# Three pairs of cms chunks with their down projections by seven products per pair

## The chip, the cores and the metric

The kernel runs on one core of one Trainium2 chip. The metric is the device time of one execution in microseconds (us). TensorE is called PE here (its sequencer starts one matmul after the other), VectorE DVE, ScalarE ACT, GpSimd POOL and SyncE SP. SP issues nearly all the transfers.

## The reference, cut to what matters

Four blocks run one after the other over x (4 batches of 512 tokens of width 512). Blocks 0 and 2 are the "cond" blocks, 1 and 3 are adapters with a layer norm. The part in question is the cms perceptron of a cond block:

```python
attn_out = jnp.einsum('btT,bTd->btd', attn, v) @ Wp + bp
cms_out = jax.nn.gelu(attn_out @ cW1 + cb1, approximate=False) @ cW2 + cb2   # 512 -> 2048 -> 512
cms_out = cms_out + target_embed
concat = jnp.concatenate([attn_out, cms_out], axis=-1)
modifier = jax.nn.gelu(concat @ mW1 + mb1, approximate=False) @ mW2 + mb2    # 1024 -> 2048 -> 512
out = jnp.clip(x + cms_out + modifier, 0.0, 1.0)
```

All is fp32.

## The kernel before

**Rounds and slots.** Two batches and one layer pair (a cond block and its adapter) are one round; there are 4 rounds (2 layers x 2 groups of batches). A round has the attention, then 16 slots, then the adapter. The hidden width of 2048 is cut into 8 chunks of 256. Slots 0 to 7 are the chunks of cms, slots 8 to 15 those of the modifier.

**Precision by halves.** Each fp32 operand is held as a high part in fp32r and a low part (the rest). ACT writes the high part with a copy, DVE subtracts it from the original and writes the low part. A product of two such operands is three matmuls (high x high, high x low, low x high), each of 128 x 128 weights by 512 columns, as lines 615 to 617 of `tile` issue them.

**Seven products.** The two batches of a round and the halves of the weights form 2 x 2 block matrices, which are multiplied by seven products instead of eight. The weights' sums S1 to S4 are made by POOL (`sums`, line 551 and on, 128 x 256 each). The products are Q1 to Q7. An up projection of slots 1 to 15 goes that way: seven products of 6 matmuls in the cms slots (A alone), of 12 in the modifier's (A and C). In slots 8 to 14 the down projection does, too (`down_product`): its operands are sums of the hidden tiles, made by POOL (`hidden_sum`, lines 563 to 575, 128 x 512 each), and its results are added up by DVE two tiles at a time (`seven_add`, lines 1474 to 1480). The down projection of the cms slots is plain (`down`): 8 output tiles, each of 2 parts, 48 matmuls a slot, and DVE adds each tile (`down_add`, line 1493).

**A cms slot.** PE goes through Q1, Q5, Q6, Q2, Q7 of chunk n, then the first batch's down projection of chunk n - 1, Q4, Q3, and the second batch's. ACT copies finished products from bank to bank as the start of others (`take`, line 1091), applies the gelu (line 1098), and makes the high parts of hidden tiles (`hidden_hi`, line 1103) and of weights (`split_hi`, line 955). DVE makes the low parts (`hidden_lo`, line 1517; `split_lo`, line 1321), the adds, and the sums of two products (`combine`, line 1504).

**Orders.** Each engine has its own list, written out by hand, and executes it in order; semaphores tie them together. An engine that waits holds up all that stands behind in its list. PE's products wait for `w_lo` (the low part of the weights), for `h_lo` (of the hidden tile) and for `added` (the bank has been drained).

**Weights.** SP loads them into three stage buffers. In the cms slots the up weights of chunk n (A) take stage 0 or 1 by turns and the down weights (D) stage 2. A load waits until the last low part has been made of what the buffer held. From the stage, ACT and DVE write both parts into a ring, from where PE reads.

Of the kernel before, what the change touches and what calls it, by code (L numbers as in the profile page):

```python
# [9 lines left out]
P = 128  # L10
D = 512
T = 512
# [18 lines left out]

BP, CB1, CB2, MB1, MB2 = 0, KT, KT + HID // P, 2 * KT + HID // P, 2 * KT + 2 * HID // P
# [7 lines left out]
LASTS = (CH - 1, SLOTS - 1)  # L40

# [17 lines left out]
UP_ORDER = ((Q1, Q5, Q6, Q2, Q7, Q4, Q3), (Q1, Q5, Q6, Q2, Q3, Q7, Q4))  # L59

DOWN_ORDER = ((Q1, Q5, Q6, Q3, Q7, Q4, Q2), (Q1, Q5, Q6, Q3, Q7, Q2, Q4))

DRAIN = {Q1: (0, 0), Q2: (0, 0), Q5: (1, 2), Q6: (1, 0), Q3: (1, 0), Q7: (1, 2), Q4: (0, 2)}
LAST_DRAIN = {(0, 0): Q2, (0, 2): Q4, (1, 0): Q3, (1, 2): Q7}
FIRST_DRAIN = (Q1, Q5, Q6, Q4)

# [14 lines left out]

RING_A, RING_C, RING_DQ = ring_of("A"), ring_of("C"), ring_of("D")
# [15 lines left out]
HID_SUMS = (T1, T3, T2, T4)  # L98
CMS_T = {T1: 2, T2: 3, T3: 4, T4: 5}
# [14 lines left out]

def seven(n):

    return CH <= n < SLOTS - 1


def amid(n):  # L120

    return CH < n < SLOTS - 1
# [14 lines left out]
DOWN_BEFORE, ROUND_DOWNS = counts(lambda n: PRODUCTS if seven(n) else GROUP * KT)  # L137
HID_BEFORE, ROUND_HIDDEN = counts(lambda n: PRODUCTS if seven(n) else 4)
ROUND_HSUMS = len(HID_SUMS) * (SLOTS - 1 - CH)

SPLIT = ((0, 1, 2, 3), (0, 3, 1, 2))
# [6 lines left out]
def weight_stream():  # L148
# [18 lines left out]
    def down(r, n):  # L167
        pieces.append(((r, "D", n), 2))
        ops.append((r, "D", n))

# [9 lines left out]
    for r in range(ROUNDS):  # L180
# [4 lines left out]
        for n in range(CH):  # L185
            if n and n - 1 not in LASTS:
                down(r, n - 1)
            up(r, n + 1, 0)
            if n in LASTS:
                down(r, n)  # L190
            up(r, n + 1, 1)
# [26 lines left out]
for piece_key, stage_at in PIECES:  # L218

    stage_loads[stage_at] += 2 if piece_key[1] in ("A", "C") else 1  # L220
    STAGE_NTH[piece_key] = stage_loads[stage_at]
    STAGE_FREE[piece_key] = LAST_OP[stage_held[stage_at][-1]] if stage_held[stage_at] else N_FOLD
    stage_held[stage_at].append(piece_key)

SUMMED = []
for sum_r in range(ROUNDS):
    for sum_n in range(1, CH):
        SUMMED.append((sum_r, "A", sum_n))
    SUMMED += [(sum_r, "A", CH), (sum_r, "C", CH)]
# [8 lines left out]
def build(nc, x_t, codes, roles, fold_w, cms_w, mod_w, ada_w, vecs, avecs, out):  # L238
# [3 lines left out]
    with ctx:  # L242
# [18 lines left out]
        vc = place("vc", [P, XTILES, T], F32R)  # L261
        pc = place("pc", [P, GROUP, KT, T], F32, at=vc_at + HI_AT[T3] * tile_bytes)
# [6 lines left out]
        stage = [place(f"stage{n}", [P, STAGE_BLOCKS, BLK]) for n in range(3)]  # L269
        fold_staging = place("fold_staging", [P, 4, PIECE], F32, at=stage_at)  # L270
# [92 lines left out]

# [1447 lines left out]
```

## Time and profile before

| | |
|---|---|
| median of 3 runs | 2157.89 us (2156.2 to 2160.65) |
| the profiled execution, its time | 2156.44 us |
| the profiled execution, span of the trace | 2154.8 us |
| granted clock of TensorE, mean | 0.998 |
| busy: PE, DVE, ACT, POOL | 98%, 71%, 48%, 28% |
| matmuls | 9256 |

The span runs from the first to the last instruction of one execution. Busy times leave out waits and the issue of transfers. Two instructions of one engine that follow each other overlap a little in the records, so that the durations of many add up to slightly more than the busy time. In rows of grouped instructions the numbers after the bar are the busy time in us, the mean of one in ns, and the idle time in front of them.

### The profile page before, as it was taken

Reading aid. Unit: us, or ns where it says so; the run is one execution under the profiler, and the core shown is the slowest. Engines: PE = TensorE matmul, PEld = TensorE weight load, DVE = VectorE, ACT = ScalarE, POOL = GpSimd, SP = SyncE. Lnnn points to the kernel's source line nnn. Section 1 sums busy time; section 2 is a strip of 40 time slices with the busy share of each in tenths; the row PEclk is TensorE's granted clock in tenths of the full one; section 3 lists DMA queues with packets and bytes.
Section 4 is the critical chain, followed back from the end, with each engine's and each line's share of the span. In section 5 each row is a group of like instructions: output and inputs, shape, how many; then the busy total and the mean of one; then the engine's idle time right before and its main releaser. Section 6 shows DMA issues by size and latency. Waiting matters only on the chain.

```text
span 2154.8 us, 24846 instructions
## 1 busy us (share of the span) xinstructions
PE 2105.6 (98%) x9256; PEld 1724.7 (80%) x9256; DVE 1537.7 (71%) x1923; ACT 1042.1 (48%) x1527; POOL 598.7 (28%) x620
## 2 busy tenths in 40 slices
PE   8999999999999999999999999999999999999997
PEld 6888887888788887888877888788887888878884
DVE  4366678776867668876776766977686866787676
ACT  5264445454446444544554544444454644454444
POOL 1001136452001113655000111655400011355420
PEclk9999999999999999999999999999999999999999
DMA  8101131212202112221312111321130211311211
GB/s 304 40 10 59 59 88 49 59 48 78 100 20 88 59 59 69 59 59 59 116 41 88 40 59 42 96 59 59 40 127 20 102 46 59 88 50 59 59 59 39
DMA packets 125767, 146.41 MB, mean 68 GB/s; under 512 B 5952, under 2 KB 100160, under 8 KB 123728
## 3 DMA queue, kind: packets, MB, share of 16 engines
q1 hardware_dynamic: 122912, 130.05, 18.9%
q0 software_dynamic: 1504, 8.49, 1.9%
q10 hardware_dynamic: 1232, 6.29, 0.7%
q8 instruction: 74, 1.21, 0.2%
q14 instruction: 45, 0.37, 0.1%
HBM read 123.84 MB, written 12.58 MB: 63 GB/s over the span
## 4 chain that ended last, share of the span: by engine, by line
PE 85%; DVE 10%; ACT 2%; issue 2%; DMA 0%; SPq 0%; ACTq 0%; DVEq 0%
PE bank L615 28%; PE bank L617 28%; PE bank L616 28%; DVE ring L1321 2%; DVE vc L1363 2%; DVE pc L1493 1%; DVE xa L1358 1%; DVE lsum L1695 1%; ACT ring L955 1%; ACT raw L1098 0%; PE bank L923 0%; DVE xs L1700 0%; DVE xs L1653 0%; DVE xs L1685 0%; DVE raw L1439 0%
## 5 line engine op out<-in xcount | busy, mean ns | idle before, releaser
L1321 DVE TENSOR_TENSOR ring<-stage,ring 128x1024 fp32r<-128x1024 f32 (+1 forms) x312 | 363.4, 1176 | 103.8 <-ACT ring L955 103.6
L551 POOL TENSOR_TENSOR stage<-stage 128x256 f32<-128x256 f32 x120 | 106.3, 886 | 1122.1 <-DMA stage<-cms_w 904.5
L615 PE MATMUL bank<-ph_hi,ring 128*128 128x512 f32 x1048 | 410.6, 392 | 5.4 <-issue 2.4
L617 PE MATMUL bank<-ph_hi,ring 128*128 128x512 f32 x1048 | 407.9, 389 | 0.0
L616 PE MATMUL bank<-ph_lo,ring 128*128 128x512 f32 x1048 | 407.9, 389 | 0.0
L615 PE MATMUL bank<-xa,ring 128*128 128x512 f32 x1016 | 396.0, 390 | 2.9 <-DVE xs L1653 2.1
L617 PE MATMUL bank<-xa,ring 128*128 128x512 f32 x1016 | 395.3, 389 | 0.0
L616 PE MATMUL bank<-xa,ring 128*128 128x512 f32 x1016 | 395.3, 389 | 0.0
L955 ACT ACTIVATE ring<-stage 128x1024 fp32r<-128x1024 f32 (+1 forms) x312 | 296.3, 970 | 111.7 <-PE bank L617 78.3
L615 PEld LDWEIGHTS bank<-ph_hi,ring 128*128 128x128 f32 x1048 | 196.7, 188 | 53.7 <-issue 7.2
L617 PEld LDWEIGHTS bank<-ph_hi,ring 128*128 128x128 f32 x1048 | 196.7, 188 | 41.0
L616 PEld LDWEIGHTS bank<-ph_lo,ring 128*128 128x128 f32 x1048 | 196.8, 188 | 40.8 <-issue 0.7
L1517 DVE TENSOR_TENSOR ph_lo<-raw,ph_hi 128x512 fp32r<-128x512 f32 x312 | 214.8, 711 | 17.4 <-ACT ph_hi L1103 17.3
L615 PEld LDWEIGHTS bank<-xa,ring 128*128 128x128 f32 x1016 | 190.7, 188 | 45.3 <-DVE ring L1321 5.8
L617 PEld LDWEIGHTS bank<-xa,ring 128*128 128x128 f32 x1016 | 190.7, 188 | 39.6
L616 PEld LDWEIGHTS bank<-xa,ring 128*128 128x128 f32 x1016 | 190.8, 188 | 39.4
L615 PE MATMUL bank<-vc,ring 128*128 128x512 f32 x512 | 200.4, 391 | 7.5 <-DVE ring L1321 6.1
L616 PE MATMUL bank<-vc,ring 128*128 128x512 f32 x512 | 199.3, 389 | 0.0
L617 PE MATMUL bank<-vc,ring 128*128 128x512 f32 x512 | 199.2, 389 | 0.0
L1493 DVE TENSOR_TENSOR pc<-bank,pc 128x512 f32<-128x512 f32 x224 | 152.3, 689 | 60.5 <-PE bank L617 60.2
L1103 ACT ACTIVATE ph_hi<-raw 128x512 fp32r<-128x512 f32 x144 | 87.9, 629 | 200.1 <-PE bank L617 198.5
L1504 DVE TENSOR_TENSOR raw<-bank,snap 128x512 f32<-128x512 f32 x112 | 77.2, 689 | 144.6 <-PE bank L617 140.3
(159 smaller groups left out, 3139.6 us busy)
## 6 DMA issues: line engine op xcount, KB each, us to landing
stage<-mod_w SPq DMA_DIRECT2D x128, 256.0 KB, 3.4
stage<-cms_w SPq DMA_DIRECT2D x36, 512.0 KB, 3.6
stage<-mod_w SPq DMA_DIRECT2D x32, 512.0 KB, 4.9
stage<-cms_w SPq DMA_DIRECT2D x56, 256.0 KB, 4.3
fold_staging<-fold_w SPq DMA_DIRECT2D x16, 512.0 KB, 5.2
stage<-folded SPq DMA_DIRECT2D x16, 512.0 KB, 4.3
xs<-pc POOLq DMA_DIRECT2D x8, 1024.0 KB, 8.3
stage<-ada_w SPq DMA_DIRECT2D x16, 512.0 KB, 3.6
```

The lines of the kernel that those rows point to most:

```text
L551: pool.tensor_tensor(part(S1), part(S2), part(A22), ALU.add).then_inc(sums_ready, 1)
L615: pe.matmul(dst, lh, rh, start=start and n == 0, stop=False, skip_group_check=not start)
L616: pe.matmul(dst, lh, rl, start=False, stop=False, skip_group_check=not start)
L617: done = pe.matmul(dst, ll, rh, start=False, stop=n == last, skip_group_check=not start)
L955: act.activation(ring_part(key, 0), staged(key), ACT.Copy).then_inc(w_hi, 1)
L1103: act.activation(ph_hi[:, tile, :], raw[:, tile, :], ACT.Copy).then_inc(h_hi, 1)
L1321: dve.tensor_tensor(ring_part(key, 1), staged(key), f32(ring_part(key, 0)), ALU.subtract).then_inc(w_lo, 1)
L1358: dve.tensor_tensor(xa[:, 8 + 4 * b + k:8 + 4 * b + k + 2, :], src[:, b, k:k + 2, :], f32(xa[:, 4 * b + k:4 * b + k + 2, :]), ALU.subtract ...
L1363: dve.tensor_tensor(block_lo(t, blk, j, n), src, f32(block_hi(t, blk, j, n)), ALU.subtract).then_inc(lo_sem, 1)
L1493: done = dve.tensor_tensor(acc, src, acc, ALU.add)
L1504: dve.tensor_tensor(raw[:, to, :], bank[BANK[q]][:, :], snap[:, 0, :], ALU.add).then_inc(combined, 1)
L1517: done = dve.tensor_tensor(ph_lo[:, at, :], src, f32(ph_hi[:, at, :]), ALU.subtract)
```

## The change

Chunks 0 to 5 of cms are taken in three pairs. The down projection of a pair is one 2 x 2 block product (batches by hidden halves: chunk 2i and chunk 2i + 1) and goes by seven products of 2 tiles x 2 parts x 3 = 12 matmuls. Chunks 6 and 7 keep the plain down projection.

- **PE.** In an odd slot (n = 2i + 1) it goes through Q5, Q1 of the up projection, the pair product Q7 of the pair before, Q6, Q2, pair Q4, Q3, pair Q2, Q7, then pair Q1 of its own pair, Q4, pair Q5. In an even slot: Q5, Q1, pair Q3, Q6, Q2, Q3, Q7, pair Q6, Q4. An odd slot has 102 matmuls (66 in slot 1), an even one 66. Slot 7 finishes pair 2 and does chunks 6 and 7.
- **Hidden sums.** POOL makes T1 to T4 of a pair, 8 sums of 128 x 512. Chunk 2i + 1 has its own hidden tiles `raw_odd`. ACT and DVE split 14 tiles per pair where they split 8. The high part of the second tile of T4, the fourth sum, stands behind the copy of Q6 in ACT's list.
- **Weights.** The pair's down weights are a piece "E" of 7 blocks of 128 x 512 across stages 1 and 2, loaded by 4 transfers of 256 KB (`load_pair`). POOL makes four sums of 128 x 512 of them, ACT and DVE split it in four parts of 2, 1, 2 and 2 blocks. The up weights A of all cms chunks now pass through stage 0 alone, which P holds before A of chunk 1.
- **DVE** drains a product two tiles at a time (`pair_add`), 7 per pair in place of 16 adds.

The core of the diff; the lists of ACT, DVE and PE for the slots:

```diff
-        pieces.append(((r, "A", n), n % 2 if n < CH else 0))
+        pieces.append(((r, "A", n), 0))
...
+            def load_pair(r, n):
+                sp.wait_ge(w_lo, STAGE_FREE[r, "E", n])
+                for c, blocks in ((n - 1, (PAIR_AT[A11], PAIR_AT[S4])), (n, (PAIR_AT[A12], PAIR_AT[A22]))):
...
+                    for m, to in enumerate(blocks):
+                        sp.dma_start(stage_pair[:, to, :].rearrange("p (k n) -> p k n", k=2), src[:, :, m, :]).then_inc(stage_in[1], 16)
...
+                for n in range(1, CH):
+                    i = n // 2
+                    if n % 2 and paired(n):
+                        pair_sum(r, i, T1, 0)
+                        pair_sum(r, i, T1, 1)
+                        sums((r, "A", n + 1))
+                        for j in range(2):
+                            pair_sum(r, i, T3, j)
+                            pair_sum(r, i, T2, j)
+                    elif n % 2 == 0:
+                        pair_sum(r, i - 1, T4, 0)
+                        pair_sum(r, i - 1, T4, 1)
+                        sums((r, "A", n + 1))
+                        if paired(n):
+                            sums((r, "E", n + 1))
...
+            def pair_product(r, i, q):
+                blk, at = OPERAND[q], RING_E[q] * BLK
+                pe.wait_ge(w_lo, W_AT[r, "E", 2 * i + 1, PAIR_GROUP[q]])
+                pe.wait_ge(h_lo, pair_split_at(r, i, blk, 1))
+                before = {Q6: Q1, Q7: Q6, Q4: Q7, Q3: Q5, Q2: Q3}
+                if q in before:
+                    pe.wait_ge(added, pair_down_at(r, i, before[q]))
+                elif i:
+                    pe.wait_ge(added, pair_down_at(r, i - 1, Q4 if q == Q1 else Q2))
...
+            def pair_even(r, n):            # PE
+                i = n // 2 - 1
+                up(r, n, Q5)
+                up(r, n, Q1)
+                pair_product(r, i, Q3)
+                up(r, n, Q6)
+                up(r, n, Q2)
+                up(r, n, Q3)
+                up(r, n, Q7)
+                pair_product(r, i, Q6)
+                up(r, n, Q4)
...
+            def pair_even(r, n):            # ACT
+                i = n // 2 - 1
+                act.wait_ge(down_done, pair_down_at(r, i, Q5))
+                split_hi((r, "E", n - 1, 3))
+                split_hi((r, "A", n, 1))
+                take(r, n, Q1, bank[BANK[Q2]][:, :])
+                pair_t_hi(r, i, T3, 0)
+                pair_b_hi(r, i, B21, 1)
+                pair_t_hi(r, i, T2, 0)
+                take(r, n, Q5, snap[:, 0, :])
+                pair_t_hi(r, i, T3, 1)
+                pair_t_hi(r, i, T2, 1)
+                pair_t_hi(r, i, T4, 0)
+                take(r, n, Q6, bank[BANK[Q3]][:, :])
+                pair_t_hi(r, i, T4, 1)
+                up_turn(r, n, 0)
...
+                split_hi((r, "A", n + 1, 0))
+                up_turn(r, n, 2)
...
+                up_turn(r, n, 3)
...
+                up_turn(r, n, 1)
...
+            def pair_odd(r, n):             # ACT, first lines
+                i = n // 2
+                if i:
+                    split_hi((r, "A", n, 1))
+                if i == 0:
+                    split_hi((r, "E", n, 0))
+                    split_hi((r, "E", n, 1))
+                    act.wait_ge(gelu_done, gelu_at(r, 0, 3))
+                take(r, n, Q1, bank[BANK[Q2]][:, :])
...
+            def pair_even(r, n):            # DVE
+                i = n // 2 - 1
+                pair_add(r, i, Q5)
+                split_lo((r, "E", n - 1, 3))
+                split_lo((r, "A", n, 1))
+                pair_split_lo(r, i, T3, 0)
+                pair_split_lo(r, i, B21, 1)
+                pair_split_lo(r, i, T2, 0)
+                pair_split_lo(r, i, T3, 1)
+                pair_add(r, i, Q3)
+                pair_split_lo(r, i, T2, 1)
+                combine(r, n, C12)
+                pair_split_lo(r, i, T4, 0)
+                combine(r, n, C22)
+                split_lo((r, "A", n + 1, 0))
+                pair_add(r, i, Q6)
+                pair_split_lo(r, i, T4, 1)
+                if paired(n):
+                    pair_split_lo(r, i + 1, B11, 0)
...
+            def pair_odd(r, n):             # DVE
+                i = n // 2
+                if i:
+                    split_lo((r, "A", n, 1))
+                    pair_split_lo(r, i, B11, 1)
+                    pair_add(r, i - 1, Q7)
+                pair_split_lo(r, i, T1, 0)
+                pair_split_lo(r, i, T1, 1)
+                split_lo((r, "E", n, 0))
+                split_lo((r, "E", n, 1))
+                split_lo((r, "A", n + 1, 0))
+                if i:
+                    pair_add(r, i - 1, Q4)
+                combine(r, n, C12)
+                combine(r, n, C22)
+                pair_split_lo(r, i, B22, 0)
+                if i:
+                    pair_add(r, i - 1, Q2)
+                pair_split_lo(r, i, B21, 0)
+                split_lo((r, "E", n, 2))
+                pair_add(r, i, Q1)
+                pair_split_lo(r, i, B22, 1)
```

## Rows read from the trace of the kernel before

**Rows 1.** The page: span, busy times, and the costliest group of matmuls.
```profile
span 2154.8 us, 24846 instructions
...
PE 2105.6 (98%) x9256; PEld 1724.7 (80%) x9256; DVE 1537.7 (71%) x1923; ACT 1042.1 (48%) x1527; POOL 598.7 (28%) x620
...
L615 PE MATMUL bank<-ph_hi,ring 128*128 128x512 f32 x1048 | 410.6, 392 | 5.4 <-issue 2.4
```

**Rows 2.** Stretches: attention, a cms slot, modifier slots; columns in the first line.
```profile
core 0: us, PE busy (x) PEld busy (x) DVE busy (x) ACT busy (x) POOL busy (x), PEclk, DMA share, GB/s
630.00:640.00 10.00, 10.00 (x45) 8.26 (x45) 10.00 (x14) 3.08 (x5) 0.00 (x0) 1.00 0.01 2
...
718.20:738.60 20.40, 20.40 (x92) 16.90 (x91) 12.59 (x18) 9.55 (x15) 3.24 (x4) 1.00 0.17 52
...
880.00:1050.00 170.00, 170.00 (x751) 140.81 (x751) 123.08 (x135) 81.72 (x121) 80.96 (x85) 1.00 0.19 56
```

**Rows 3.** Waits of PE: us in total, times, longest.
```profile
PE bank L615 <- DVE ring L1321: 8.9, 16, 1.5
...
PE bank L654 <- DVE pc L1340: 3.0, 3, 1.0
```

**Rows 4.** Groups of DVE's instructions in two cms slots, 718 to 758.8 us.
```profile
L1493 DVE TENSOR_TENSOR pc<-bank,pc 128x512 f32<-128x512 f32 x17 | 11.7, 690 | 5.7 <-PE bank L617 5.6
L1517 DVE TENSOR_TENSOR ph_lo<-raw,ph_hi 128x512 fp32r<-128x512 f32 x8 | 5.5, 703 | 0.0
L1321 DVE TENSOR_TENSOR ring<-stage,ring 128x1024 fp32r<-128x1024 f32 x4 | 4.9, 1222 | 2.0 <-ACT ring L955 2.0
L1504 DVE TENSOR_TENSOR raw<-bank,snap 128x512 f32<-128x512 f32 x4 | 2.8, 692 | 8.1 <-PE bank L617 8.1
L1321 DVE TENSOR_TENSOR ring<-stage,ring 128x768 fp32r<-128x768 f32 x2 | 1.9, 957 | 0.4 <-ACT ring L955 0.4
```

**Rows 5.** Groups of ACT's instructions in the same two slots.
```profile
L1103 ACT ACTIVATE ph_hi<-raw 128x512 fp32r<-128x512 f32 x10 | 6.0, 628 | 17.2 <-PE bank L617 17.1
L955 ACT ACTIVATE ring<-stage 128x1024 fp32r<-128x1024 f32 x4 | 4.2, 1060 | 1.3 <-PE bank L617 1.3
L1098 ACT ACTIVATE raw<-raw,vec 128x512 f32<-128x512 f32 x4 | 2.9, 716 | 1.6 <-DVE raw L1504 1.6
...
L1091 ACT ACTIVATE bank<-bank 128x512 f32<-128x512 f32 x4 | 2.3, 582 | 1.8 <-PE bank L617 1.8
```

**Rows 6.** A group of POOL's sums of weights in the same two slots.
```profile
L552 POOL TENSOR_TENSOR stage<-stage 128x256 f32<-128x256 f32 x2 | 1.5, 738 | 0.0
```

**Rows 7.** Timeline of DVE and POOL: start, duration in us, then the instruction.
```profile
828.43 4.54 DVE L1363 TENSOR_TENSOR vc<-pc,vc 128x1024 fp32r<-128x1024 f32 x2 [1.13 <-ACT vc L981]
866.62 2.31 DVE L1321 TENSOR_TENSOR ring<-stage,ring 128x1024 fp32r<-128x1024 f32 x1
...
828.46 1.05 POOL L551 TENSOR_TENSOR stage<-stage 128x256 f32<-128x256 f32 x1
...
831.97 1.60 POOL L556 TENSOR_TENSOR stage<-stage 128x256 f32<-128x256 f32 x1
...
866.18 1.67 POOL L575 TENSOR_TENSOR raw<-raw 128x512 f32<-128x512 f32 x1 [1.23 <-DVE ph_lo L1517]
```

**Rows 8.** Timeline of DVE, SP and POOL in a modifier slot, 898 to 908 us.
```profile
898.98 0.94 DVE L1321 TENSOR_TENSOR ring<-stage,ring 128x768 fp32r<-128x768 f32 x1
...
901.10 1.23 DVE L1480 TENSOR_TENSOR xs<-bank,xs 128x1024 f32<-128x1024 f32 x1 [1.18 <-PE bank L617]
...
899.95 1.21 SPq L443 DMA_DIRECT2D stage<-mod_w  x2
...
904.01 0.74 POOL L551 TENSOR_TENSOR stage<-stage 128x256 f32<-128x256 f32 x1 [5.50 <-DMA stage<-mod_w]
...
907.05 1.29 POOL L563 TENSOR_TENSOR raw<-raw 128x512 f32<-128x512 f32 x1
```

**Rows 9.** Timeline of ACT where slot 1 begins.
```profile
677.25 1.14 ACT L1103 ACTIVATE ph_hi<-raw 128x512 fp32r<-128x512 f32 x2
678.29 0.59 ACT L1091 ACTIVATE bank<-bank 128x512 f32<-128x512 f32 x1
```

More of the change, by code:

```diff
@@ L184, in weight_stream @@
         plain(r, "P", 0)
-        for n in range(CH):
-            if n and n - 1 not in LASTS:
-                down(r, n - 1)
-            up(r, n + 1, 0)
-            if n in LASTS:
-                down(r, n)
-            up(r, n + 1, 1)
+        up(r, 1, 0)
+        ops.append((r, "A", 1, 1))
+        for n in range(1, CH - 1):
+            if n % 2 == 0:
+                ops.append((r, "E", n - 1, 3))
+            if n > 1:
+                ops.append((r, "A", n, 1))
+            if n % 2:
+                pair_first(r, n)
+                ops.append((r, "E", n, 1))
+            up(r, n + 1, 0)
+            if n % 2:
+                ops.append((r, "E", n, 2))
+        ops.append((r, "A", CH - 1, 1))
+        down(r, CH - 2)
+        staged_up(r, CH)
+        ops.append((r, "A", CH, 0))
+        down(r, CH - 1)
+        ops += [(r, "C", CH, 0), (r, "A", CH, 1), (r, "C", CH, 1)]
         up(r, CH + 1, 0)
@@ new lines, in pair_add @@
+            def pair_add(r, i, q):
+                b, m = DRAIN[q]
+                acc, src = pc[:, b, m:m + 2, :], pair[int(q in (Q5, Q3, Q2))]
+                minus = q in (Q5, Q7, Q4)
+                dve.wait_ge(down_done, pair_down_at(r, i, q))
+                if q not in PAIR_FIRST_DRAIN:
+                    dve.wait_ge(added, pair_down_at(r, i, {Q2: Q1, Q6: Q3, Q7: Q5}[q]))
+                elif i:
+                    dve.wait_ge(added, pair_down_at(r, i - 1, PAIR_LAST_DRAIN[b, m]))
+                if i == 0 and q in PAIR_FIRST_DRAIN:
+                    dve.wait_ge(attn_lo, (r + 1) * ATT_BUILDS)
+                    for j in range(2):
+                        done = dve.tensor_scalar(acc[:, j, :], src[:, j, :], -1.0 if minus else 1.0,
+                                                 cbias[:, 2 * r + b, m + j:m + j + 1], ALU.mult, ALU.add)
+                elif minus:
+                    done = dve.tensor_tensor(acc, acc, src[:, :, :], ALU.subtract)
+                else:
+                    done = dve.tensor_tensor(acc, src[:, :, :], acc, ALU.add)
+                done.then_inc(added, 1)
@@ L1593, in slot @@
-                up_lo(r, n + 1, 1)
-                if not last:
-                    for m in range(1, KT):
-                        down_add(r, n - 1, 1, m)
+                for m in range(KT):
+                    down_add(r, n - 1, 1, m)
+                hidden_lo(r, n, 3)
+                split_lo((r, "C", n + 1, 0))
+                hidden_lo(r, n, 1)
+                combine(r, n, C12)
+                hidden_lo(r, n, 2)
+                split_lo((r, "A", n + 1, 1))
+                split_lo((r, "C", n + 1, 1))
```

379 lines of the change are left out of this document (277 added, 102 removed).

## The prediction, made before the result was known

> **What bounds the kernel now.** I read the page's busy line first, then the stretches of the profile cut at the slots of the cms half, then the waits of PE. The page has PE busy for 98% of the span, DVE for 71%, POOL for 28% [rows 1]. The stretches show that the part being changed is the densest there is: a cms slot lasts 20.40 us and PE is busy for all 20.40 of them, at a granted clock of 1.00 [rows 2]. A slot before the change has 42 matmuls of its up products and 48 of the down projection, 90 in all, so one matmul costs 20.40 / 90 = 0.2267 us (the 92 of the row are starts counted at the cut; the 392 ns of one matmul [rows 1] overlap with its neighbours', so they are not its price). All the waits of PE that the trace names are small: the largest sum is 8.9 us in 16 waits over the whole span [rows 3]. So PE's instruction count sets the time here, and removing matmuls pays in full as long as no other engine becomes late. In the same slot DVE is busy for 12.6 us, ACT for 9.6, POOL for 3.3 [rows 2]. The reader should see that there is room on three engines, and that the change spends it.
>
> **What it removes.** Six of the eight cms chunks of a round are taken in pairs. Two plain down projections are 2 x 8 tiles x 2 parts x 3 = 96 matmuls. Seven products per pair are 7 x 2 x 2 x 3 = 84. That is 12 fewer per pair, with 3 pairs in each of 4 rounds 144 fewer: 144 x 0.2267 = 32.6 us. A pair's two slots have 168 matmuls and need 38.1 us of PE where they took 40.8. The up products are only reordered.
>
> **What it adds, per pair.** Durations are of one instruction.
> DVE before: splits of A 2 x (1.22 + 0.96), two of D at 1.22, 8 hidden splits of 0.69, 16 adds of 0.69, 4 combines of 0.69 [rows 4]: 26.2 us, and busy 25.2 (two slots) [rows 2], since neighbours overlap by a few per cent. After: A 4.4, four splits of E (three of 1024 columns, one of 512) 4.3, 14 hidden splits 9.7, seven double adds of 1.22 [rows 8] 8.5, 4 combines 2.8: 29.7, that is about 28 busy of 38.1.
> ACT [rows 5]: splits of A 3.8, of E 3.8, 14 copies of 0.63, 8 gelus of 0.7, 6 copies out of PSUM of 0.58: 25.5, so about 24 of 38.1.
> POOL: 8 sums of A of 0.74 [rows 6], 4 sums of E of twice the width, 8 hidden sums. The nearest row to a sum of 512 columns undisturbed is 1.29 [rows 8]. So 5.9 + 12 x 1.29 = 21.4 against 6.5 before.
> DMA: a pair's weights come in 4 transfers of 256 KB instead of 2 of 512 KB, the same bytes, which cost SP about 0.6 us each to issue [rows 8]; the DMA share is 0.17 [rows 2], so the bytes are hidden. Round edges: the load of A1 now waits for the split of P, with the pair's load and the residual's traffic queued behind it on SP; A1 is needed some 25 us later, so it costs nothing by itself.
> By these sums no engine passes PE. The question is whether they add.
>
> **Where they don't add.** When POOL sums overlap a DVE instruction with both inputs in SBUF, one waits for the other. A split of 1024 columns takes 1.22 alone and 2.31 beside the hidden sum that began 0.44 us before it [rows 4, 7]: 1.09 for a POOL sum of 512 columns. Two DVE splits beside four POOL sums of 256 took 4.54 where two take 2.45 [rows 4, 7]: 0.52 per sum. DVE's adds and combines read PSUM and keep their length beside POOL. The Trainium skill, page SBUF — State Buffer, section "SBUF: two separate sides", says it as a rule: DVE with two SBUF inputs and GpSimd take one port pair by an exclusive lock for a whole instruction. The trace agrees with the page, by those two rows; the sum by the durations alone, without the lock, would be the rival "hidden" below.
> A pair has 12 POOL sums of 512 columns and 8 of 256: 12 x 1.09 + 8 x 0.52 = 17.2 us that DVE may wait. DVE's own SBUF part (all splits, 18.4 less overlap) is 17.3 of 38.1, 45%. If POOL's sums fell at random, DVE would wait 0.45 x 17.2 = 7.8. In the modifier slots, built the same way, a slot of 126 matmuls (28.56 us) has 4 x 1.09 + 12 x 0.52 = 10.6 at risk. DVE's durations there (six weight splits 6.5, seven hidden 4.8, seven double adds 8.5, two combines 1.4) are 21.3, less overlap 20.0, and the row says 123.08 / 170 x 28.56 = 20.7 [rows 2]: it loses 0.7, and PE is busy for 170.00 of 170. So the bounds of the wait are 1.1 (that share) and 17.2 (all), and DVE's fill is 29 to 45 of 38.1. The port alone carries 17.3 + 17.2 = 34.5 of 38.1, where a modifier slot has 10.6 + 10.6 of 28.56. I take a wait of 8: DVE at 36 of 38.1, which is full enough that orders fixed in advance bring PE to a stop at the tight places. These are:
> First, the even slot is only 66 matmuls, 15.0 us, and the next chunk's A must pass through one stage buffer in it (before, cms chunks alternated between two). From the start of DVE's split that frees the buffer to POOL's first sum on the new data it is 904.01 - 898.98 = 5.0 us [rows 8]. Added to it: three POOL sums 2.3, ACT's split 1.05, DVE's 1.22: 9.6. The freeing split stands behind a double add and E's last split, 1.2 + 1.2 after PE ends the odd slot, and up to 1.1 for the sum of T4; the sums of A may meet two hidden splits, 1.4; and in two even slots of three E's wide sums start just when DVE comes to the split of A, 1.1 or, two in a row, 2.2. So the new A is ready at 12.0 when nothing meets and at 16.7 when all does, with 15.0 allowed: a stall of 0 to 1.7. I take 1.0, nearer to all than to nothing, because these pieces follow each other in a fixed order and meet each time or never.
> Second, the product by T2 (Q6) needs the eighth split of DVE's even slot, behind the add of Q3: 0.3.
> Third, adds in the odd slot stand in DVE's queue behind the wait for the split of A, whose load is late by what E's sums cost: products Q4 and Q1, 0.3.
> Together some 1.6 us per pair (1.0 + 0.3 + 0.3), 12 x 1.6 = 19. In the first slot two E splits stand before the copy of Q1, 1.05 + 0.6 where 1.14 stood [rows 5, 9]: 0.5 later, half hidden, 4 x 0.2 = 1, within the rounding.
>
> **The sum.** 32.6 - 19 = 13.6 less. The profiled execution has a span of 2154.8 and a time of 2156.4: 2142.8. The median shown, 2157.9, is 1.5 above that execution, so 2144.
>
> **Rivals.**
> *Hidden.* The orders of the queues fit, as in the modifier slots, and only about 1 us in all is lost: 2157.9 - 32.6 + 1 = 2126, up to 2132. For it: the 100% busy PE of the modifier slots with DVE at 72%. Against it: port and POOL are far fuller here. 20%.
> *Cancelled.* Stalls of 2.4 to 3.1 us per pair, which is what 2.72 per pair gives within 4.3 / 12: 2154 to 2162. 13%.
> *The port binds, slower.* Nearly each POOL sum meets a DVE split, because DVE, once late, always has one waiting. Then a pair lasts as long as DVE: 28 + 0.85 x 17.2 = 42.6, against 40.8 before: 12 x 1.8 = 22 more, 2180 at worst, about 2168 if it holds for half the pairs. It decides from a stall of 2.7 us per pair on. Against it: DVE waits for PSUM results at its combines (8.1 us in two slots now [rows 4]), and POOL can catch up there without meeting it. 15%.
> *Attention.* A1's and E1's sums move into the stretch after P's split, where DVE is busy for 10.0 of 10 us and the matmul after it waits 1 us for it [rows 2, 3]. Bound: 4 x 0.52 + 4 x 1.09 = 6.4 per round in three rounds, 19 us; below: nothing, as half of DVE's work there reads PSUM. I take 0 to 1 per round. It shifts each case and is none by itself. The sums that now run in slot 0 leave it, but PE does not wait there, so nothing is gained.
>
> **Chances and range.** A measurement tells about 0.2%, 4.3 us, from no change. The likeliest, stalls of 0.6 to 2.4 us per pair, has 52% and its own range is 2132 to 2153. Faster: 0.52 + 0.20 = 0.72. Same: 0.13. Slower: 0.15. From the full saving to the edge of the slower case is 2126 to 2162, which leaves out some 5% below and 15% above.
>
> **What would show it.** Matmuls 9112 instead of 9256; pairs of slots of 38.1 us plus stalls, to be read off PE's waits, whose releaser should be DVE's split of A (L1321's successor) at the start of odd slots; DVE's split of 512 columns above its 0.69; POOL busy up by about 12 x 15 = 180 us. If DVE's means stay as they are and PE has no new waits, the lock was priced too high and the time is 2126. If the wait before PE is on ACT's copies, I named the wrong engine.

## The result, and the profile after

| | before | after |
|---|---|---|
| median | 2156.2 us (5 runs, 2155.07 to 2160.65) | 2169.9 us (5 runs, 2165.7 to 2171.37) |
| profiled execution: time, span | 2156.44, 2154.8 | 2165.7, 2163.9 |
| granted clock, mean | 0.998 | 0.995 |

The ratio is 1.0057, with a 95% interval of 1.0041 to 1.0073: the change makes the kernel slower, by 12.3 us by this ratio (the medians lie 13.7 apart). The forecast was 13.6 us less.

The page of the kernel after, against [rows 1]:

```profile
span 2163.9 us, 24878 instructions
...
PE 2093.5 (97%) x9112; PEld 1697.2 (78%) x9112; DVE 1673.8 (77%) x1927; ACT 1094.5 (51%) x1623; POOL 843.7 (39%) x764
...
L1614 DVE TENSOR_TENSOR ring<-stage,ring 128x1024 fp32r<-128x1024 f32 (+1 forms) x288 | 373.3, 1308 | 108.3 <-ACT ring L1169 108.0
```

The 144 matmuls are gone. DVE has four instructions more than before and is busy for 136 us more (1537.7 before), POOL for 245 us more.

Where the time went is read by cutting the span at two instructions of each round, ACT's first gelu of slot 0 and its first copy in slot 8. The differences of their start times in the timeline, one number for each round:

| | before | after |
|---|---|---|
| cms slots (first gelu to copy in slot 8) | 178.6, 180.4, 178.7, 178.8 | 178.6, 178.5, 179.6, 180.1 |
| the rest up to the next round's first gelu | 340.2, 340.2, 339.9 | 345.0, 341.6, 342.6 |

The four rounds of cms slots add up to 716.5 before and 716.7 after. So all 32.6 us that the missing matmuls give back are lost inside the slots, and 0.2 more: 32.9 us (before rounding) in 12 pairs, 2.7 per pair. The three stretches between them, with the adapter and the attention, add 8.9 us. (In every kernel's trace some rounds come to the copy in slot 8 about 1.7 us later than others, counted from the start of that slot: one of four before, two of four after. Without that the loss is 2.6 per pair. What makes them late was not looked into.) Together that is 9.1, which is what the span has grown by (2163.9 - 2154.8).

Slots 3 and 4 of round 1, as a stretch (columns as in [rows 2]), cut at ACT's copy of Q5 in slot 3 and in slot 5, about 4 us behind the start of the slot; and the longest of PE's waits in slots 1 to 6 of that round, where the kernel before has none that the trace names:

```profile
717.54:758.54 41.00, 39.80 (x170) 31.01 (x169) 36.89 (x35) 23.27 (x37) 27.87 (x21) 1.00 0.18 52
```

```profile
PE bank L768 <- DVE ring L1614: 1.4, 2, 0.9
PE bank L768 <- DVE pc L1883: 0.8, 2, 0.6
PE bank L768 <- DVE pc L1886: 0.3, 2, 0.2
```

(This view counts an idle time between the modelled end of a matmul and the start of the next, and leaves out the short ones. The distances between the starts of matmuls, used further down, show more.)

The pair takes 41.0 us where 168 matmuls need 38.1, and DVE is busy for 36.9 of them. It is not full, and PE stops all the same, seldom for long. The same stretch by form, DVE and then POOL:

```profile
L1614 DVE TENSOR_TENSOR ring<-stage,ring 128x768 fp32r<-128x768 f32 x3 | 6.1, 2047 | 0.0
L1866 DVE TENSOR_TENSOR ph_lo<-raw,ph_hi 128x512 fp32r<-128x512 f32 x4 | 5.2, 1293 | 0.1
L1614 DVE TENSOR_TENSOR ring<-stage_pair,ring 128x1024 fp32r<-128x1024 f32 x3 | 5.1, 1709 | 0.3 <-ACT ring L1169 0.3
L1888 DVE TENSOR_TENSOR pc<-bank,pc 128x1024 f32<-128x1024 f32 x4 | 4.8, 1210 | 0.0
L1614 DVE TENSOR_TENSOR ring<-stage,ring 128x1024 fp32r<-128x1024 f32 x2 | 3.3, 1626 | 2.8 <-ACT ring L1169 2.8
L1866 DVE TENSOR_TENSOR vc<-raw_odd,vc 128x512 fp32r<-128x512 f32 x4 | 2.9, 724 | 0.0
...
L1794 DVE TENSOR_TENSOR raw<-bank,snap 128x512 f32<-128x512 f32 x2 | 1.4, 678 | 0.0
```

```profile
L712 POOL TENSOR_TENSOR raw_odd<-raw_odd 128x512 f32<-128x512 f32 x2 | 4.0, 1976 | 2.1 <-DVE vc L1866 2.1
...
L669 POOL TENSOR_TENSOR stage<-stage 128x256 f32<-128x256 f32 x2 | 2.9, 1448 | 0.0
...
L668 POOL TENSOR_TENSOR stage<-stage 128x256 f32<-128x256 f32 x2 | 1.9, 930 | 2.1 <-DMA stage<-cms_w 2.1
```

Most splits, with both inputs in SBUF, are longer than in [rows 4]: 768 columns take 2.05 for 0.96, 1024 take 1.6 to 1.7 for 1.22, 512 take 1.29 for 0.70 in one group and 0.72 in another. The adds and combines, with one input in PSUM, keep their 1.2 and 0.68. POOL's sums are longer too: T4's 1.98 for 1.29, a weight sum of 256 columns 1.45 for 0.74. And DVE, though late, sits idle for 2.8 us in front of the split of A (2.0 before): it waits for ACT's half, which waits for POOL's sums. These wait 2.1 us for the load of A, and then DVE's splits hold them up. The timeline of one such meeting, at the end of slot 4 and where slot 5 begins (754.48):

```profile
748.88 1.18 POOL L669 TENSOR_TENSOR stage<-stage 128x256 f32<-128x256 f32 x1
...
750.13 1.14 POOL L671 TENSOR_TENSOR stage<-stage 128x256 f32<-128x256 f32 x1
...
751.30 1.06 ACT L1169 ACTIVATE ring<-stage 128x1024 fp32r<-128x1024 f32 x1 [2.41 <-POOL stage L671]
...
752.05 1.29 POOL L668 TENSOR_TENSOR stage_pair<-stage_pair 128x512 f32<-128x512 f32 x1
...
752.40 2.03 DVE L1614 TENSOR_TENSOR ring<-stage,ring 128x1024 fp32r<-128x1024 f32 x1 [1.13 <-ACT ring L1169]
...
753.30 2.27 POOL L669 TENSOR_TENSOR stage_pair<-stage_pair 128x512 f32<-128x512 f32 x1
...
754.48 0.50 PE L768 MATMUL bank<-xa,ring 128*128 128x512 f32 x1 [0.54 <-DVE ring L1614]
```

Two sums of A are stretched (1.18 and 1.14 for 0.74), DVE idles 1.13, its split meets the first sum of E (2.03 for 1.22), the second sum of E meets the split (2.27 for 1.29), and PE stands.

In the stretch after the attention's start, the stop is larger. PE's waits over the span, against [rows 3]:

```profile
PE bank L768 <- DVE ring L1614: 12.4, 18, 1.5
PE bank L807 <- DVE pc L1633: 10.3, 3, 4.1
```

The three waits of the transposes for DVE were 3.0 us and are 10.3. The timeline of DVE and POOL before the longest of them:

```profile
637.40 1.28 POOL L668 TENSOR_TENSOR stage_pair<-stage_pair 128x512 f32<-128x512 f32 x1 [1.46 <-DMA stage_pair<-cms_w]
...
638.38 4.89 DVE L2070 TENSOR_SCALAR xs<-xs,avec 128x512 f32<-128x512 f32 x4
...
638.65 1.48 POOL L669 TENSOR_TENSOR stage_pair<-stage_pair 128x512 f32<-128x512 f32 x1
...
640.21 1.35 POOL L671 TENSOR_TENSOR stage_pair<-stage_pair 128x512 f32<-128x512 f32 x1
...
641.64 1.35 POOL L673 TENSOR_TENSOR stage_pair<-stage_pair 128x512 f32<-128x512 f32 x1
```

The four operations that finish the norm took 1.82 us before (line 1706 there, at 639.52) and take 4.89 beside the four sums of E. They have one tensor input, in SBUF. After the stop of 4.1 us, which ends at 649.34, the granted clock is half for some us, as two overlapping stretches show:

```profile
648.00:655.00 7.00, 5.66 (x22) 5.21 (x23) 6.71 (x14) 4.12 (x8) 0.00 (x0) 0.51 0.29 109
650.00:660.00 10.00, 10.00 (x43) 8.69 (x42) 5.91 (x11) 3.65 (x6) 0.00 (x0) 0.76 0.56 198
```

### The profile page after: what moved, and what is told of

It reads as the page before. It is cut to its first block, busy times and chain, and to the rows that moved or that the text cites. A ratio compares the mean times of both kernels' runs of the same rounds, so it can differ in the third digit from the quotient of the medians.

```text
span 2163.9 us, 24878 instructions
## 1 busy us (share of the span) xinstructions
PE 2093.5 (97%) x9112; PEld 1697.2 (78%) x9112; DVE 1673.8 (77%) x1927; ACT 1094.5 (51%) x1623; POOL 843.7 (39%) x764
## 4 chain that ended last, share of the span: by engine, by line
PE 69%; DVE 17%; ACT 4%; issue 3%; DMA 3%; POOL 3%; SPq 1%; ACTq 0%; DVEq 0%; POOLq 0%
PE bank L768 23%; PE bank L769 22%; PE bank L770 22%; DVE ring L1614 5%; DVE vc L1656 2%; DMA stage<-cms_w 2%; ACT ring L1169 1%; DVE ph_lo L1866 1%; DVE pc L1781 1%; DVE pc L1888 1%; ACT raw L1312 1%; DVE lsum L2059 1%; DMA stage_pair<-cms_w 1%; DVE xa L1651 1%; DVE pc L1883 1%
## 5 line engine op out<-in xcount | busy, mean ns | idle before, releaser
L1614 DVE TENSOR_TENSOR ring<-stage,ring 128x1024 fp32r<-128x1024 f32 (+1 forms) x288 | 373.3, 1308 | 108.3 <-ACT ring L1169 108.0
L1169 ACT ACTIVATE ring<-stage 128x1024 fp32r<-128x1024 f32 (+1 forms) x288 | 271.2, 963 | 156.7 <-POOL stage L671 82.2
L768 PE MATMUL bank<-ph_hi,ring 128*128 128x512 f32 x808 | 319.5, 395 | 9.7 <-DVE pc L1883 3.0
L770 PE MATMUL bank<-ph_hi,ring 128*128 128x512 f32 x808 | 315.1, 390 | 0.0
L769 PE MATMUL bank<-ph_lo,ring 128*128 128x512 f32 x808 | 315.0, 390 | 0.0
L768 PE MATMUL bank<-vc,ring 128*128 128x512 f32 x704 | 277.3, 394 | 11.3 <-DVE ring L1614 6.1
L770 PE MATMUL bank<-vc,ring 128*128 128x512 f32 x704 | 274.5, 390 | 0.0
L769 PE MATMUL bank<-vc,ring 128*128 128x512 f32 x704 | 274.4, 390 | 0.0
L768 PEld LDWEIGHTS bank<-xa,ring 128*128 128x128 f32 x1016 | 190.8, 188 | 62.5 <-DVE ring L1614 13.9
L769 PEld LDWEIGHTS bank<-xa,ring 128*128 128x128 f32 x1016 | 190.9, 188 | 38.5
L768 PEld LDWEIGHTS bank<-ph_hi,ring 128*128 128x128 f32 x808 | 151.7, 188 | 55.7 <-issue 20.0
L770 PEld LDWEIGHTS bank<-ph_hi,ring 128*128 128x128 f32 x808 | 151.7, 188 | 31.9
L769 PEld LDWEIGHTS bank<-ph_lo,ring 128*128 128x128 f32 x808 | 151.8, 188 | 30.9 <-issue 0.7
L768 PEld LDWEIGHTS bank<-vc,ring 128*128 128x128 f32 x704 | 132.2, 188 | 49.4 <-issue 9.2
L1807 DVE TENSOR_TENSOR ph_lo<-raw,ph_hi 128x512 fp32r<-128x512 f32 x216 | 148.6, 712 | 16.0 <-ACT ph_hi L1317 16.0
L1773 DVE TENSOR_TENSOR xs<-bank,xs 128x1024 f32<-128x1024 f32 x104 | 126.7, 1218 | 43.1 <-PE bank L770 42.8
L770 PEld LDWEIGHTS bank<-vc,ring 128*128 128x128 f32 x704 | 132.2, 188 | 27.9
```

The lines of the kernel that those rows point to most:

```text
L768: pe.matmul(dst, lh, rh, start=start and n == 0, stop=False, skip_group_check=not start)
L769: pe.matmul(dst, lh, rl, start=False, stop=False, skip_group_check=not start)
L770: done = pe.matmul(dst, ll, rh, start=False, stop=n == last, skip_group_check=not start)
L1169: act.activation(ring_part(key, 0), staged(key), ACT.Copy).then_inc(w_hi, 1)
L1614: dve.tensor_tensor(ring_part(key, 1), staged(key), f32(ring_part(key, 0)), ALU.subtract).then_inc(w_lo, 1)
L1773: done = dve.tensor_tensor(acc, src[:, :, :], acc, ALU.add)
```

## The experiments

Each was measured together with the kernel before, and its ratio is to those runs. Stretches and pairs are read off each one's own trace, as above.

**1. The sums out of the attention.** One wait holds the four sums of E1 until the norm's last operation is done.

```diff
                 sums((r, "A", 1))
+                if r:
+                    pool.wait_ge(x_final, r * GROUP * KT)
                 sums((r, "E", 1))
```

> The changed kernel with one wait more: in rounds 1 to 3 POOL starts the sums of the first pair's down weights only when DVE has finished the norm's last scaling. Theory A (the sums of the first pair collide with DVE's scaling in the attention, PE stops for 4.1 us there and TensorE's clock halves for some us after it): DVE's four scalings go back from 4.9 to 1.8 us, PE's wait before the transposes from 4.1 to 1.0 us, no stretch at half clock, and the kernel is 9 to 12 us faster than the changed one (8.9 us lie between the slots of one round and of the next in its trace), so about equal to or up to 5 us slower than before. Rival (the attention is slow because the loads queue behind each other on SP, or for another reason): no change, within 2 us.

Measured: 2157.58 us (10 runs), ratio 1.0001 (0.9991 to 1.0011), level with before and 12 less than the changed kernel, as expected. The three stretches are 339.3 each, the norm's operations are back to their length, and the clock stays at full speed. Timeline of DVE, and PE's waits:

```profile
639.84 1.82 DVE L2072 TENSOR_SCALAR xs<-xs,avec 128x512 f32<-128x512 f32 x4
```

```profile
PE bank L809 <- DVE pc L1635: 2.9, 3, 1.0
```

The cms slots add up to 716.8 us, as in the changed kernel: their loss is another one, and it is whole.

The stretches are 0.9 us shorter than those of the kernel before, and its trace has a likely reason. There POOL made the sums of A1 (581.56 to 586.5) beside two of DVE's splits, ahead of a stop of PE:

```profile
581.70 3.37 DVE L1358 TENSOR_TENSOR xa<-pc,xa 128x1024 fp32r<-128x1024 f32 x2 [0.26 <-ACT xa L978]
...
587.51 0.50 PE L615 MATMUL bank<-ring,xa 128*128 128x512 f32 x1 [1.08 <-DVE xs L1685]
```

In the changed kernel these sums come later, the two splits take 2.4 and the stop is gone. So E1's sums cost more than the 8.9 us that the stretches have grown by: 1029.2 - 1017.9 = 11.3 us, of which 2.4 are covered by this gain. No run moves A1's sums alone.

**2. Hidden sums that hardly read.** The eight hidden sums of a pair work on 64 of their 512 columns.

```diff
-pool.tensor_tensor(raw[:, j, :], raw[:, j, :], raw[:, 2 + j, :], ALU.subtract)
+pool.tensor_tensor(raw[:, j, 0:64], raw[:, j, 0:64], raw[:, 2 + j, 0:64], ALU.subtract)
```

> The changed kernel, POOL's eight hidden sums of a pair computed on 64 of 512 columns only (the rest of the sum is left out). All waits, splits and matmuls stay. Theory P (DVE and POOL take turns on a port, and DVE's lateness stops PE in the pairs' slots): each such sum takes 1.1 us less from DVE wherever they meet; some 4 to 5 meet per pair, so the pair in the middle goes from 41.0 us to 39.0 to 40.0 and the kernel is 12 to 24 us faster than the changed one. Rival L (the load of A through the single stage buffer is what is late): POOL's hidden sums are not on that chain except for one, so at most 0.5 us per pair, 6 us. Rival D (DVE's own longer list is the cause): no change.

Measured: 2140.64 us, ratio 0.9926 (0.991 to 0.9943). The pair in slots 3 and 4 takes 38.08, with no stop of PE, and the cms slots add up to 688.5 us, 28 less than after. By the medians the kernel is 29 us faster than the changed one, where 12 to 24 were expected. The stretches with the attention stay slow (341.5, 341.3, 343.0).

**3. Weight sums that hardly read.** The four sums of E work on 64 of 512 columns; three more transfers of 256 KB per pair fill the places of the sums.

```diff
+                cols = slice(0, 64 if key[1] == "E" else BLK)
...
-                    return s[:, at[block], :]
+                    return s[:, at[block], cols]
```

> The changed kernel, POOL's four sums of a pair's down weights on 64 of 512 columns (the rest of the sum is left out), and the three blocks that they would fill are loaded as copies by three more transfers of 256 KB. Theory A and P: the attention gets its 9 us back (no collision of 512 columns), and in two slots of three in a round DVE's split of the next A is not held by 0.9 us, nor the two splits after it by 1.1 each: 8 x 1 to 1.5. Together 15 to 22 us faster than the changed kernel. Rival L: the three transfers more on SP make nothing faster, attention apart: 9 us faster or less.

Measured: 2137.62 us, ratio 0.991 (0.9894 to 0.9927). The pair takes 38.1 to 38.6, the attention stretches are at 339.3. The cms slots add up to 698.7 us, 18 less than after. By the medians the kernel is 32 us faster than the changed one, where 15 to 22 were expected.

**4. Both.** Experiments 1, 2 and 3 in one kernel.

> Both of the two kernels before it in one, and the first sums held: all POOL sums of 512 columns of the pairs on 64 columns. Theory P: nearly the whole saving of 32.6 us appears, 2124 to 2134. Rival L (single stage buffer): PE still stops at the start of odd slots by 1 us or more, and with what else hangs on the loads 12 to 20 us of the saving stay lost, 2138 to 2145. Rival D (DVE's longer list): 2145 or more.

Measured: 2126.56 us, ratio 0.986 (0.9843 to 0.9876). This is as expected. Slots 3 and 4, and 5 and 6, take 38.08 in every round. The cms slots add up to 686.8, that is 29.7 less than before; 1.7 of the 2.9 that lack to 32.6 is one more round that comes to slot 8's copy 1.7 later. A still goes through one stage buffer here, and DVE's list is as long as in the changed kernel. The same two slots:

```profile
702.71:740.79 38.08, 38.08 (x170) 31.54 (x169) 30.29 (x34) 23.29 (x38) 12.94 (x20) 1.00 0.25 77
```

**5. Write without reading.** On experiment 1, each of the 12 sums of 512 columns is a fill of the same tile, which reads nothing (0.53 us for 1.29).

```diff
-pool.tensor_tensor(raw[:, j, :], raw[:, j, :], raw[:, 2 + j, :], ALU.subtract)
+pool.memset(raw[:, j, :], 0.5)
```

> The kernel of e1 (first sums held), with all twelve POOL sums of 512 columns of a pair as fills with a constant over the full 512 columns: they write and read nothing from SBUF (the sums are left out). Theory P1 (it is the read port: DVE with two SBUF inputs and a POOL instruction that reads take turns): DVE's splits keep their 0.69 and 1.22 us beside them, and the kernel lands near e4, 2125 to 2132. Theory P2 (any POOL instruction on SBUF, writing too, holds DVE up): splits stay long, in proportion to the length of the fills. Rival W (not the port but POOL's own 1.3 us per sum, on which ACT's copies wait): if a fill takes as long as a sum, 2145 or more; if it is much shorter this run can't tell it, only DVE's durations can.

Measured: 2124.87 us, ratio 0.9834 (0.9814 to 0.9854), the pair at 38.08. DVE's split is back to its length beside them:

```profile
L1868 DVE TENSOR_TENSOR ph_lo<-raw_odd,ph_hi 128x512 fp32r<-128x512 f32 x24 | 16.4, 683 | 3.4 <-ACT ph_hi L1398 3.4
```

**6. The split of T4's second tile earlier.** In the changed kernel ACT makes it behind the copy of Q6; here in front of it.

```diff
                 pair_t_hi(r, i, T4, 0)
-                take(r, n, Q6, bank[BANK[Q3]][:, :])
                 pair_t_hi(r, i, T4, 1)
+                take(r, n, Q6, bank[BANK[Q3]][:, :])
```

> The changed kernel with the one line moved back: ACT's copy of the second tile of T4 stands before the copy of Q6. In the changed kernel's trace the sum of T4 ends 1.7 us after ACT starts the copy of Q6, so ACT waits that long and PE's Q3 with it, in 12 even slots: theory (in-order queue on the path): 12 x 1.2 to 1.7 = 14 to 20 us slower than the changed kernel. Rival (the stalls only move: DVE catches up while PE waits, and later stalls shrink by as much): less than 8 us slower.

Measured: 2173.35 us, ratio 1.0064 (1.0043 to 1.0084), about level with the changed kernel (1.0057) and not the 14 to 20 us slower that the theory gave. The copy, which PE's next product starts from, comes 1.7 us late, but then the odd slots start without a stop in every round. Timeline of PE:

```profile
749.70 0.47 PE L768 MATMUL bank<-xa,ring 128*128 128x512 f32 x1 [1.67 <-ACT bank L1305]
```

The pair is 41.1 for 41.0: while PE waits for one thing, DVE and POOL work off what the next stop would have been. Here a stop of PE did not add its length to the time, because other stops shrank.

**7. and 8. The same sums at other times.** On experiment 1, POOL makes only the first sum of E in the even slot and the other three in the odd slot behind T1; the splits of E's middle parts and of the next A stand later in both lists. Experiment 8 also has POOL wait for DVE's split of A before that first sum.

```diff
                         pair_sum(r, i, T1, 1)
+                        if i:
+                            sums((r, "E", n), (1,))
                         sums((r, "A", n + 1))
...
+                            pool.wait_ge(w_lo, W_AT[r, "A", n + 1, 0])
-                            sums((r, "E", n + 1))
+                            sums((r, "E", n + 1), (0,))
```

> An attempt at a faster order, on top of e1: of a pair's four sums of down weights POOL makes only the first in the even slot, the other three in the odd slot behind T1; DVE's and ACT's splits of the next A, of the pair's S4 and of A12, A22 move behind the copies and adds that PE needs first. All work is done. Theory P: the splits at the change of slots (A's first part, two hidden ones, A's second part) meet one sum of 512 columns instead of four, 2 to 3 us of DVE per pair; the pair of 41.0 us goes to 39.5 to 40.3 and the kernel to 2140 to 2150. Rival (the port is short in total, wherever the sums stand, they meet splits): within 4 us of e1.

> As e7, and the first of these sums waits until DVE has split the next A's first part, so that this split is never behind it. Theory P: PE's stop of 0.8 to 1.1 us at the start of two odd slots of a round goes, 8 x 0.8 = 6 us at most, less what it costs after; 2 to 6 us faster than e7. Rival as in e7: no difference from e7, as the collision only moves to the next split.

Measured: 2153.56 us (10 runs), ratio 0.9978 (0.9968 to 0.9987), and 2149.68, ratio 0.9953 (0.9937 to 0.9969). The pair in slots 3 and 4 takes 39.0 to 40.2, then 39.2 to 39.4. The same work at other times gives, by the ratios against experiment 1, 5 and 10 us back of 33: part of the loss is a matter of who meets whom. Experiment 7 had been expected at 2140 to 2150 and missed it; it lies between the theory and its rival. Experiment 8 is 4 us below experiment 7, within the 2 to 6 expected.

**9. Fills as long as the sums.** On experiment 5, three fills per sum, each waiting for the one before, so that POOL is as busy as in the changed kernel (836.2 us over the span, 843.7 there).

> As e5, each sum of 512 columns now as three fills one after the other, each over the full 512 columns and waiting for the one before: 3 x 0.53 + 2 x 0.08 = 1.75 us where a sum takes 1.3 alone and 1.3 to 2.3 beside DVE. POOL reads nothing in them (the sums are left out). Theory P1 (the read port): DVE's splits keep their lengths and PE stays full: 2124 to 2132. Rival W (POOL's time per sum, on which ACT and so DVE and PE wait): stalls as in e1, 2145 to 2160, with DVE's splits at 0.69.

Measured: 2126.94 us, ratio 0.9847 (0.9832 to 0.9862), the pair at 38.08. The same two slots:

```profile
705.73:743.80 38.07, 38.07 (x170) 31.53 (x169) 29.60 (x34) 23.31 (x37) 27.32 (x45) 1.00 0.19 57
```

POOL is busy for 27.3 us, as after (27.9), DVE for 29.6 instead of 36.9, and PE never stops. What costs is what POOL reads beside DVE, not how long its work takes: every wait, split and matmul of experiment 1 is still there. The Trainium skill, page SBUF — State Buffer, section "Who interferes with whom", says that DVE with two SBUF inputs contends with a GpSimd instruction that reads SBUF and not with one that only writes it; experiments 5 and 9 agree.

**10. The single stage buffer.** On experiment 1, A of chunks 3, 5 and 7 isn't loaded: POOL makes its sums of what the buffer holds, as soon as the split before has left it. What is left out is those three chunks' own up weights and their transfers; every other instruction stays.

```diff
+                if n in (3, 5, 7):
+                    return
```

> The kernel of e1 with the loads of A for chunks 3, 5 and 7 left out: POOL takes its sums in place of what stage 0 still holds, as soon as DVE has split it, so about 4 us earlier in each of the three even slots (the weights of these chunks are then not the right ones). Theory P: POOL's sums are earlier, but as many meet DVE: within 6 us of e1, either way. Rival L (the single stage buffer, my prediction's first tight place): the stop of PE at the start of odd slots goes, and the pair falls by 1 us: 10 to 14 us faster than e1.

Measured: 2145.41 us, ratio 0.9941 (0.9925 to 0.9956), 12 below experiment 1. The pair is at 40.15, DVE nearly as busy as in experiment 1 (37.0 for 37.9), and slot 5 starts without a stop. So leaving out the reload gives 12 us by the medians, 9 in the slots of the profiled executions, which is what the rival (the single stage buffer) had forecast, and not theory P. But it can't be the cause by itself: in experiments 4, 5 and 9 the reload is there and costs nothing. It counts only once the sums have made DVE late. POOL's sums of A also come at another time here and meet other splits, and no run parts that from the time of the load.

**11. Four more moves in the lists.** On experiment 8: the low part of T2's second tile before the add of Q3, the one of B22's second tile before E's third split (in ACT's list too), and in slot 1 the two combines together.

> e8 with four moves in the lists, all work done: DVE splits the second tile of T2 before it adds Q3; in slot 1 it makes C22 right behind C12; the second tile of B22 is split before the last part of E, on ACT and DVE. In e8 PE still stops for 0.5 to 0.6 us before the product Q6 in three slots of a round, for 1.2 us before Q4 and 0.8 us before the first Q3 in the slots 1 and 2. Theory P: these stops shrink to less than half, 12 x 0.4 + 4 x 1.2 = 10 us at most, 4 to 8 us faster than e8: 2142 to 2146. Rival (stops only move): within 2 us of e8.

Measured: 2147.6 us, ratio 0.9946 (0.9932 to 0.9959), level with experiment 8, as the rival had it. The pair in slots 3 and 4 is down to 38.5 to 38.9. But slots 1 and 2 (from copy to copy) take 34.9 in three of the four rounds, where they took 33.6 to 34.4 in experiment 8. Timeline of PE there:

```profile
693.71 0.47 PE L776 MATMUL bank<-ph_hi,ring 128*128 128x512 f32 x1 [2.03 <-DVE pc L1890]
```

PE comes to the first pair's product Q3 earlier and waits 2.0 us for DVE, which has to add Q5 first. In round 1 the granted clock then falls for some matmuls (last section), which costs 1.6 us more. Of the kernels that do all the work, experiments 8 and 11 are the best of the study: 0.5% below the kernel before, 1% below the changed one.

## Why the prediction was wrong

**Matmuls and their price: right.** 9112 matmuls are left, and with the port left alone (experiments 4, 5, 9) the kernel is at 2124.9 to 2126.9, 31 to 33 us below the runs of before that go with it. That is the *hidden* case, 2126: 32.6 us less about 1 for the first slot. The slots lose 1.2 of them, at the same places in experiments 2, 4, 5 and 9. That the time fits to the microsecond is in part luck, since one to two more rounds with a late slot 8 (1.7 each) and the stretches shorter by 2.7 were not forecast.

**The lock: right in kind and in size.** That DVE's splits and POOL's sums hold each other up was forecast, and experiments 1, 5 and 9 show it. I took a wait of 8 us per pair for DVE. DVE is busy for 36.9 us of the pair's two slots in the changed kernel and 37.9 in experiment 1; where the wide sums read nothing it is 30.5 and 29.6 (experiments 5 and 9). So they cost 6.4 to 8.3. The 1.09 us per wide sum hold as well: a split of 512 columns at 222.33, beside one sum of T4 that began 0.45 us before it, takes 1.77 us for 0.68.

**The step that failed: "Together some 1.6 us per pair (1.0 + 0.3 + 0.3)".** It measured 2.7 (32.9 / 12). The sum has only the three places that I could name as tight, and every other place at nothing. PE's stops can be placed by the distances between the starts of its matmuls. As far as these exceed 0.2267 us, they add up in slots 1 to 7 of the four rounds to 35.4 us, and to 4.2 in the kernel before: 31.2 more, 2.6 per pair. The rest to 2.7 is the one more round with a late slot 8. Experiment 9, with the same matmuls and nothing wide read by POOL, has 5.4. The 30.0 us above it, by the product before which they stand, per pair:

| place | forecast | measured |
|---|---|---|
| start of the odd slot (in slot 7 also Q1) | 1.0 | 0.7 |
| pair product Q6, by T2 | 0.3 | 0.5 |
| pair products Q4 and Q1 in the odd slot | 0.3 | 0.2 |
| pair product Q3 in the even slot | 0 | 0.5 |
| Q3 of the up projection in the odd slot | 0 | 0.4 |
| pair product Q5 at the end of the odd slot | 0 | 0.15 |

The three places that I named lost 1.4, slightly less than forecast. The others lost 1.1, and they are what is missing. The largest, in each of the 12 even slots, is the pair product Q3: its bank has to be drained of Q5, the last product of the slot before, and PE is there after only 12 matmuls, 2.7 us. The next stands in three odd slots of eight, 1.0 to 1.1 us before Q3 of the up projection, for ACT's copy of Q6, and exactly in those that had no stop at their start, so it looks like the same lateness at another place. Timeline of PE, in slot 2 of round 1 and slot 5 of round 0:

```profile
699.77 0.47 PE L768 MATMUL bank<-ph_hi,ring 128*128 128x512 f32 x1 [0.61 <-DVE pc L1883]
...
242.38 0.47 PE L768 MATMUL bank<-xa,ring 128*128 128x512 f32 x1 [0.93 <-ACT bank L1305]
```

At the first place, from the freeing split to the end of the split of the next A, it took 754.43 - 741.99 = 12.4 us in round 1, where I had 9.6 and up to 3.6 of meetings; slots 3, 5 and 7 of that round start 1.1, 0.8 and 0.6 us late, the last of them 6 matmuls in and for ACT's gelu.

DVE's fill was a little low too. Its own work I had put at 28 busy of 38.1, from durations of 29.7 less an overlap; it is 29.6 to 30.5 (with what A's sums still cost it). That made 36.9 to 37.9, not 36. The slots 3 and 4 of round 1 over all the kernels:

| kernel | DVE busy in the pair | pair, 38.1 needed |
|---|---|---|
| experiment 9 | 29.6 | 38.1 |
| experiment 4 | 30.3 | 38.1 |
| experiment 5 | 30.5 | 38.1 |
| experiment 2 | 32.1 | 38.1 |
| experiment 3 | 33.9 | 38.2 |
| experiment 11 | 34.8 | 38.5 |
| experiment 8 | 35.2 | 39.3 |
| experiment 7 | 35.6 | 40.1 |
| experiment 6 | 36.4 | 41.1 |
| after | 36.9 | 41.0 |
| experiment 10 | 37.0 | 40.1 |
| experiment 1 | 37.9 | 41.2 |

Up to 34 us the lists absorb nearly everything in these two slots; between 35 and 38 they lose 1 to 3. Had I had this table, my own 36 would have read 2 to 3. The fill alone doesn't decide: experiments 6 and 10 lie out of the order. Experiments 2 and 3 say the same in another way: either half of the sums taken away gives most of the slots' loss back (28 and 18 us of 30), more together than there is. I priced the places that I could name. A late DVE is late everywhere.

**The second step that failed: "I take 0 to 1 per round" for the attention.** The profiled execution lost 8.9 us there, 3.0 per round, which is inside the bound that I had given (19 us) and not in what I took. Experiment 1 gives 12 us of the medians back. I had let the lock touch only half of DVE's work there, "as half of DVE's work there reads PSUM", and treated the rest as diluted. But the four sums of E fell on the four operations of the norm, one upon the other, and made them 3.1 us longer in round 1, just ahead of what PE waited for; the stop of PE then cost again at half clock. The Trainium skill, page SBUF — State Buffer, section "Who interferes with whom", names tensor_scalar among the operations that can contend with GpSimd, so by the page these four were to be counted, which my rule of two SBUF inputs left out; the trace (4.89 for 1.82) agrees with it.

**The sum with both.** 2142.8 for the profiled execution, plus 32.9 - 19 = 13.9, plus 8.9 is 2165.6; it took 2165.7. Both terms are read from that one trace, so they have to fit. The median of the changed kernel is 4.2 us above its profiled execution, and no trace says where these lie.

**Which rival it was.** *The port binds, slower* (15%) for the slots, as it decides "from a stall of 2.7 us per pair on", with *attention* on top. By its letter it is only half right: a pair does not last as long as DVE is busy (41.0 against 36.9), because DVE idles, 2.8 of these 4.1 us before the split of A. The queues' order binds, at a fill that the port makes. The argument against it, that DVE waits for PSUM results at its combines and POOL can catch up there, failed: those waits are gone (8.1 us in [rows 4], none at the combines after).

**What would show it.** The releaser was DVE's split of A, as named, but for two starts of odd slots only in round 1, 2.0 us of the 9.0 that the distances show in slots 1 to 7 (1.1 of the 9.0 are in the kernel before, too). ACT's copy was the releaser in three slots of the whole kernel, so DVE was not the only engine to be named. The split of 512 columns went above 0.69 (1.29), POOL's busy time by 245 us instead of 180, since its sums wait too. What stays open is which meetings of DVE and POOL make each of these stops; no run takes them one by one.

## What to carry to other kernels

Price a shared port by the pairs of instructions that the fixed orders bring together, not by a random share: four POOL sums on four DVE operations ahead of a wait of PE cost 3.1 us of their 5.2 in round 1, and lengthened the stop of PE by 1.9 to 3.1 us in each of three rounds. Leave an engine with a list in fixed order some room in the stretch that it must fit in. Here slots 3 and 4 (round 1) lost 0.1 us with DVE busy for 33.9 of 38.1 and 1.2 with 35.2; other lists will have another edge, as slots 1 and 2 of experiment 3 show, which lost 1.3 us with DVE busy for 25.6 of 31.5. Beyond it small stops appear at many places, and moving work between them gives back only part. Look first at a product that stands close behind the one whose bank it needs drained. And before trading matmuls for sums on POOL, run the kernel once with the sums made narrow: it tells in one run what the trade can give at best, and what the sums cost.

## What was unexpected of the hardware

- A TENSOR_SCALAR of 128 x 512 fp32 with one tensor input in SBUF takes 0.46 us alone (1.82 for four) and 1.2 (4.89 for four) beside POOL's sums.
- After a stop of PE of 4.1 us the granted clock was 0.51 over the 7 us from 648 on, the lower level of 1.2 GHz; round 3 had it after 2.9 us, more briefly (0.76 over 7 us), round 2 not at all after 3.3 (1.00). In experiment 11 a stop of 2.0 us was followed by this:

```profile
693.70:698.00 4.30, 4.29 (x12) 3.42 (x13) 4.30 (x5) 2.21 (x5) 1.07 (x2) 0.63 0.02 5
```

- Fills by POOL, which with A's small sums keep it busy for 27.3 us of 38.1 (experiment 9), leave PE without a stop and the means of DVE's 512-column subtractions of two SBUF tensors at 0.68 to 0.73.
